# Sixteen key projections of an attention moved into the Mamba stage before it, with the first transfers reordered

## The chip, the cores and the metric

The kernel runs on one core of one Trainium2 chip, as one launch. The metric is the device time of that launch in microseconds (us), lower is better. Everything is float32 except a few bfloat16 operands named below. TensorE (PE) multiplies, ScalarE (ACT), VectorE (DVE) and GpSimd (POOL) do the elementwise work, and SyncE (SP) and ACT issue the transfers.

## The reference, cut to what matters

The network has four pairs of layers on `x` (4 batches, 256 tokens, 256 features); the change touches the first layer and the third. `ctx` is (4, 256, 128).

```python
# layer 0: Mamba on ctx; its output is gated by the normalised x
u = silu(causal_conv4(ctx @ in_proj.T) + conv_b)        # 256 channels
dt_low, Bm, Cm = split(u @ x_proj.T, [8, 16, 16])
dt = softplus(dt_low @ dt_proj.T + dt_b);  A = -exp(A_log)
for n in range(16):                                     # states
    h_t = exp(dt*A[n]) * h_{t-1} + dt*u*Bm[n]           # a scan over the 256 tokens
    y  += h * Cm[n]
x = x + tanh(g[0]) * (y + D*u) * silu(layernorm(x))
# layer 1: dense feed-forward (width 704) on layernorm(x)
# layer 2 (first attention): 16 heads of width 128
xn = layernorm(x);  q = rmsnorm(xn @ Wq) * gq;  k = rmsnorm(ctx @ Wk) * gk
v = ctx @ Wv;  x = x + tanh(g[1]) * softmax(q k^T / sqrt(128)) v @ Wo
# then: 16 experts, a second attention, 8 experts, a quantised layer, a layer on chosen tokens
```

The keys `ctx @ Wk` depend on inputs alone, not on the layers before.

## The kernel before

Tokens are worked on in two halves of 512 (two batches each), channels in two chunks of 128. One on-chip buffer, the arena, is divided by hand for each stage. Each engine runs a program in an order written out by hand: `tensor_program`, `scalar_program` and so on call the stages one after another. Semaphores named by event (`tick`, `at`) hold an engine until another has done something. Nothing is reordered by a scheduler, so an instruction that waits holds all that stand behind it on its engine.

**Mamba** (`mamba_pe`, `mamba_act`, `mamba_dve`, `mamba_pool`) has a beginning and then 32 steps: step s works on half s // 16 and state s % 16. The beginning: SP and ACT issue the input transfers; DVE multiplies the input projection by the four taps (L739); PE does the convolution of the first half with the products, 8 matmuls (L445); ACT applies silu (L561); PE projects (L456); ACT copies the 8 rows of dt (L568, `low`). From there follow the softplus and the first scan. The gates silu(layernorm(x)), one activation for each of 8 tiles (L573), need x's statistics (DVE, L222), and a power and a product on POOL; five of them stand between the two silus and two behind. POOL then builds the selecting matrices with one CAST (L405).

In step s, PE spreads the rows B and C of the next state over the partitions (L480, two bf16 matmuls into banks 0 and 1) and adds two earlier products into the sum y (L486, identity times a 128x512 tile, two of them). ACT copies C (L633, `Cs`), in odd steps B too (L629, `Bs`), and makes the decays of both chunks in PSUM (L645, `dA`). DVE multiplies the input (L765, `dBu`; in odd steps POOL makes chunk 1's, L412) and scans both chunks (L772). POOL multiplies states by C (L420, `HC`). There are two buffers for Cs and two for the states, so Cs of step s waits for HC of step s-2, the decays of step s stand behind it on ACT, and HC waits for the add two steps earlier. Between the steps stand the second half's conv, silu (step 5, with two loads of ACT's function table and one gate), projection, softplus (steps 8 to 14), and the first half's end (`gated`, `turned`, `added`, L719, L495, L729, steps 17 to 19).

**Dense** follows on PE; the first attention's first passes stand beside its second half. **Attention 1** has 32 passes N (half N // 16, head N % 16) of two units each. For a pass, three ahead, PE projects the keys (L986, q = 0: four 128x128 blocks, bank 7) and the queries (L983, q = 1: eight matmuls, bank 6); ACT squares and copies each out (L1021, L1022); DVE sums the squares, POOL takes the root, DVE normalises both in one instruction (L1056), and PE turns them (L1007). In every unit PE does scores (L1155), a transpose of the probabilities (L1166), their product with the context (L1175) and the result (L1186); in odd units of the first half also a joined weight (L996). DVE takes the maxima (L1263) and ACT the exponentials (L1229).

Of the kernel before, what the change touches and what calls it, by code (L numbers as in the profile page):

```python
# [8 lines left out]
BF16 = mybir.dt.bfloat16  # L9
# [3 lines left out]
P = 128  # L13
B, S, D = 4, 256, 256
# [17 lines left out]
FIRST, LAST = 25392, 29952  # L32

# [275 lines left out]
class Mamba:  # L309
# [5 lines left out]
    def __init__(self, k):  # L315
        NI, NBC = self.NI, self.NBC
        k.at = 0
# [3 lines left out]
        self.taps, self.Wc = k.place(self.TAPS, NI * P), k.place(self.TAPS, NI * P)  # L321
        self.cp = k.place(B, self.TAPS - 1 + S)
        self.U, self.DT, self.DU = k.place(2, NI, HALF), k.place(2, NI, HALF), k.place(2, NI, HALF)
        self.Y = k.place(2, NI, HALF)
        self.V, self.E = k.place(NI, HALF), k.place(NI, HALF)
        self.A = k.place(NI, self.NSTATE)
        self.low = k.place(HALF)
        self.bc3 = k.place(2, HALF, dt=BF16)
        self.part = k.place(HALF, dt=BF16)
        self.bcf = k.place(HALF)  # L330
        self.sel = k.place(NBC, P, dt=BF16)
        self.row = k.place(NBC)
        self.skip = k.place(NI, P)
        self.gate = k.place(NT, S)
        self.dBu = k.place(3, HALF)
        self.Bs = k.place(HALF)
        self.Hs, self.HC = k.place(4, HALF), k.place(4, HALF)
        self.Cs = k.place(2, HALF)

# [15 lines left out]

def mamba_sp(k, m):
# [5 lines left out]
    nc.sync.dma_start(m.taps.rearrange("p w n -> p (w n)"),  # L362
                      k.io["conv_taps"].partition_broadcast(P)).then_inc(*landed("taps_in"))
# [4 lines left out]

def constants_act(k, m):
    nc, landed = k.nc, k.s.landed  # L370
    nc.scalar.dma_start(k.cols[:, :], k.io["cols"]).then_inc(*landed("cols_in"))
    nc.scalar.dma_start(m.Wx, k.io["x_proj"]).then_inc(*landed("Wx_in"))
    nc.scalar.dma_start(m.Wdt[96:96 + m.RANK], k.io["dt_proj"]).then_inc(*landed("Wdt_in"))
    nc.scalar.dma_start(k.ident[:, :], k.io["ident"]).then_inc(*landed("ident_in"))
    nc.scalar.dma_start(k.rows[:, :], k.io["rows"].partition_broadcast(P)).then_inc(*landed("rows_in"))
    nc.scalar.dma_start(m.cp[:, 2:4, m.TAPS - 1:],
                        k.io["cT"][:, HALF:T].rearrange("p (b t) -> p b t", b=2)).then_inc(*landed("cp_in1"))

# [10 lines left out]
def mamba_pool(k, m):  # L389
# [10 lines left out]
    pool.wait_ge(*at("var", "m"))  # L400
    nc.gpsimd.tensor_tensor(k.rstd[:, :], k.rstd[:, :], k.mhalf[:, 0:NT], ALU.pow).then_inc(*tick("rstd", "m"))
    pool.wait_ge(*at("rstd", "m"))
# [35 lines left out]
def mamba_pe(k, m):  # L438
# [3449 lines left out]
```

## Time and profile before

| | us |
|---|---|
| three runs | 1082.51, 1083.87, 1084.74 |
| median | 1083.87 |
| the profiled execution | 1088.27 |
| its span, first to last instruction | 1086.9 |
| PE busy | 949.8 (87%) |
| DVE, ACT, POOL busy | 723.5, 519.2, 302.4 |
| mean granted TensorE clock | 0.948 |

The profile is one execution. A PE that is "busy" includes matmuls at the lower of its two clock levels, 1.2 GHz; the granted clock says how much of full speed (2.4 GHz) it had. A float32 matmul appears as two records. The waits of an engine count only where the work behind them sets the end. By the timeline, Mamba takes the span's first 173 us, the dense layer and the first passes of attention 1 the next 79, and attention 1's last result row starts at 575.2.

### The profile page before, as it was taken

Reading aid. Unit: us, or ns where it says so; the run is one execution under the profiler, and the core shown is the slowest. Engines: PE = TensorE matmul, PEld = TensorE weight load, DVE = VectorE, ACT = ScalarE, POOL = GpSimd, SP = SyncE. Lnnn points to the kernel's source line nnn. Section 1 sums busy time; section 2 is a strip of 40 time slices with the busy share of each in tenths; the row PEclk is TensorE's granted clock in tenths of the full one; section 3 lists DMA queues with packets and bytes.
Section 4 is the critical chain, followed back from the end, with each engine's and each line's share of the span. In section 5 each row is a group of like instructions: output and inputs, shape, how many; then the busy total and the mean of one; then the engine's idle time right before and its main releaser. Section 6 shows DMA issues by size and latency. Waiting matters only on the chain.

```text
span 1086.9 us, 15034 instructions
## 1 busy us (share of the span) xinstructions
PE 949.8 (87%) x4888; PEld 682.4 (63%) x4888; DVE 723.5 (67%) x1859; ACT 519.2 (48%) x1344; POOL 302.4 (28%) x282
## 2 busy tenths in 40 slices
PE   5876769999999999999999989878589898979587
PEld 2322224567899898888986777655355556545375
DVE  3899995235666766778676544567988955567753
ACT  3673562135666666565663344355356642132331
POOL 3566783112111112136210433325231100010110
PEclk9888899999999999999999999999699999989689
DMA  8500001010111128112201535412100003211100
GB/s 294 243 1 0 0 1 48 1 30 30 46 40 34 44 56 312 41 44 99 69 2 59 175 129 182 155 50 73 49 1 1 1 1 140 79 38 40 75 20 20
DMA packets 28356, 73.96 MB, mean 68 GB/s; under 512 B 4076, under 2 KB 5366, under 8 KB 27640
## 3 DMA queue, kind: packets, MB, share of 16 engines
q1 hardware_dynamic: 24344, 63.28, 17.1%
q0 software_dynamic: 3072, 8.39, 2.4%
q10 hardware_dynamic: 864, 1.34, 0.3%
q8 instruction: 40, 0.66, 0.3%
q14 instruction: 36, 0.29, 0.1%
HBM read 50.98 MB, written 22.02 MB: 67 GB/s over the span
## 4 chain that ended last, share of the span: by engine, by line
PE 62%; DVE 15%; issue 3%; ACT 2%; SPq 1%; DMA 1%; POOL 1%; another core or an unknown queue 0%; DVEq 0%; ACTq 0%
PE psum L2093 5%; PE psum L983 5%; PE psum L1694 5%; PE psum L1175 4%; PE psum L1186 4%; PE psum L844 4%; PE psum L1155 4%; PE psum L986 3%; PE psum L1166 2%; PE psum L855 2%; PE psum L1708 2%; PE psum L1007 2%; PE psum L2112 2%; PE psum L2356 2%; PE psum L2714 2%
## 5 line engine op out<-in xcount | busy, mean ns | idle before, releaser
L1065 POOL TENSOR_TENSOR arena<-arena,mhalf 128x8 f32<-128x8 f32 x32 | 54.0, 1687 | 247.6 <-DVE arena L1050 247.6
L1287 DVE SCALAR_TENSOR_TENSOR X<-psum,arena,X 128x256 f32<-128x256 f32 x128 | 55.9, 478 | 66.0 <-PE psum L1186 63.8
L420 POOL TENSOR_TENSOR arena<-arena 128x512 f32<-128x512 f32 x64 | 82.6, 1315 | 7.3 <-DVE arena L772 6.6
L772 DVE TENSOR_TENSOR_SCAN arena<-psum,arena 128x512 f32<-128x512 f32 x64 | 74.7, 1209 | 9.6 <-ACT psum L645 8.4
L1229 ACT ACTIVATE arena<-psum,arena 128x256 f32<-128x256 f32 x128 | 60.0, 477 | 34.7 <-DVE arena L1266 32.4
L1694 PE MATMUL psum<-arena 128*128 x248 | 66.5, 391 | 10.8 <-DVE arena L1789 8.9
L2375 ACT ACTIVATE arena<-psum,arena 128x240 f32<-128x240 f32 x128 | 57.3, 463 | 33.9 <-DVE arena L2389 17.0
L486 PE MATMUL psum<-arena,ident 128*128 128x512 f32 x128 | 71.5, 681 | 1.0 <-POOL arena L420 0.7
L1186 PE MATMUL psum<-arena 128*128 128x256 f32 x256 | 66.0, 380 | 1.2 <-DVE X L1287 1.1
L1175 PE MATMUL psum<-arena 128*128 128x256 f32 x256 | 65.8, 380 | 0.0
L1155 PE MATMUL psum<-arena 128*128 128x256 f32 x256 | 65.8, 380 | 0.0
L2093 PE MATMUL psum<-xT,arena 128*128 128x512 f32 x128 | 62.2, 627 | 1.3 <-ACT arena L3158 1.2
L983 PEld LDWEIGHTS psum<-arena,xT 128*128 128x128 f32 x512 | 61.9, 192 | 1.4
L1800 DVE COPY arena<-psum 128x256 f32<-128x256 f32 x62 | 26.2, 422 | 54.7 <-PE psum L1708 42.0
L983 PE MATMUL psum<-arena,xT 128*128 128x128 f32 x512 | 62.3, 275 | 0.0
L239 POOL TENSOR_TENSOR rstd<-rstd,mhalf 128x4 f32<-128x4 f32 x14 | 14.7, 1053 | 161.5 <-DVE rstd L232 161.5
L480 PE MATMUL psum<-arena 96*128 96x512 bf16 x64 | 22.5, 434 | 38.2 <-DVE arena L765 35.7
L1021 ACT ACTIVATE arena<-psum 128x512 f32<-128x512 f32 x64 | 38.3, 598 | 35.0 <-PE psum L983 18.0
L1694 PEld LDWEIGHTS psum<-arena 128*128 128x128 f32 x248 | 42.7, 192 | 18.1 <-issue 14.7
L1241 ACT COPY arena<-psum 128x512 f32<-128x512 f32 x64 | 37.6, 588 | 33.6 <-PE psum L1166 32.4
L1155 PEld LDWEIGHTS psum<-arena 128*128 128x128 f32 x256 | 48.2, 190 | 6.6 <-issue 0.3
L2714 PE MATMUL psum<-ident,arena 128*128 128x128 f32 x256 | 38.7, 293 | 15.6 <-DVE arena L2863 6.1
(359 smaller groups left out, 2296.0 us busy)
## 6 DMA issues: line engine op xcount, KB each, us to landing
arena<-in_w SPq DMA_DIRECT2D x32, 384.0 KB, 3.1
tokens<-arena SPq DMA_DIRECT2D x2, 4096.0 KB, 23.6
arena<-tokens SPq DMA_DIRECT2D x32, 256.0 KB
results<-arena SPq DMA_DIRECT2D x32, 256.0 KB
arena<-in_moe SPq DMA_DIRECT2D x17, 384.0 KB, 3.1
arena<-in_moe SPq DMA_DIRECT2D x4, 1536.0 KB, 13.6
arena<-in_w SPq DMA_DIRECT2D x2, 1024.0 KB, 6.0
arena<-in_gu SPq DMA_DIRECT2D x1, 1280.0 KB, 6.7
```

The source lines that it names most:

```text
L420: nc.gpsimd.tensor_tensor(m.HC[:, v, :], m.Hs[:, v, :], m.Cs[:, s % 2, :], ALU.mult).then_inc(*tick("HC", s, c))
L486: nc.tensor.matmul(bank[m.bank_Y[h][c]], k.ident[:, :], m.HC[:, 2 * (s % 2) + c, :], start=False, stop=n == NSTATE - 1).then_inc(*tick("y_ ...
L772: nc.vector.tensor_tensor_scan(m.Hs[:, 2 * (s % 2) + c, :], bank[m.bank_dA[c]], input_of(m, s, c), 0.0, ALU.mult, ALU.add).then_inc(*tick( ...
L983: mm = nc.tensor.matmul(bank[b][:, j * P:(j + 1) * P], k.xT[:, c, t * P:(t + 1) * P], m.W[:, p, c * P:(c + 1) * P], start=c == 0, stop=c = ...
L1155: mm = nc.tensor.matmul(bank[w][:, j * S:(j + 1) * S], m.Q[:, N % 2, i * S + j * P:i * S + (j + 1) * P], m.K[:, N % 2, i * S:(i + 1) * S], ...
L1175: mm = nc.tensor.matmul(bank[4][:, 0:S], m.ctok[:, 2 * m.batch(u) + c, :], m.PT[:, u % 2, c, :], start=c == 0, stop=c == 1)
L1186: mm = nc.tensor.matmul(bank[5][:, j * D:(j + 1) * D], m.Z[:, u % 2, j * P:(j + 1) * P], m.M[:, h, :], start=True, stop=True)
L1229: e = nc.scalar.activation(m.Pr[:, w, j, :], bank[w][:, j * S:(j + 1) * S], ACT.Exp, bias=m.nb[:, w, j:j + 1], scale=m.SCALE, accum_out=m. ...
L1694: mm = nc.tensor.matmul(bank[b][:, 0:D], m.xgT[:, n % 2, c, :], m.W[:, bass.ds(place + c * D, D)], start=c == 0, stop=c == DC - 1)
L2093: mm = nc.tensor.matmul(bank[b], m.W[:, slot, which, c * P:(c + 1) * P], k.xT[:, c, cols], start=c == 0, stop=c == DC - 1)
L2375: nc.scalar.activation(pr[:, a, 0:KM], v[:, a, 0:KM], ACT.Exp, bias=m.nb[:, u, a:a + 1], scale=m.SCALE, accum_out=m.sums[:, a % 2, places[ ...
L2714: mm = nc.tensor.transpose(bank[4 + w][:, c * S + j * P:c * S + (j + 1) * P], m.Pr[:, u, 2 * w + j, c * P:(c + 1) * P], k.ident[:, :])
```

## The change

1. The 1 MB matrix `Wk` is loaded to the chip (`key_weights_sp`, an additional input) behind the zeroing of the token buffers, into `m.Wk`.
2. The keys of the first half, 4 token tiles by 4 groups of 4 heads, are projected by 16 matmuls of 128x512 in Mamba's steps 11 to 14, 20 to 23 and 26 to 31 (two in 26 and in 29), and each is copied by ACT one step later into `Kr`, which stays on chip. The banks are those of y: the second half's y (banks 6, 7) is started in step 16 instead of 12, and the first half's (4, 5) are free from step 20.
3. In attention 1, passes 0 to 15 have no key projection and no copy of keys; ACT squares from `Kr`, and DVE normalises keys and queries in two instructions.
4. The taps are the first transfer of ACT's queue instead of the third of SP's; `ident` goes ahead of `x_proj`, and the second half of `cT` ahead of `rows`.
5. PE does 11 matmuls of 128x128 on constants before it waits for the first input (`awake`).
6. x's statistics in Mamba are finished in two halves. Two gates stand between the first silus and one behind; two stand in step 5 and three in step 17, the latter with two table loads of its own. In steps 5 and 17 all of this stands behind the decays of the step instead of ahead of them, and Cs of the next step stands behind that step's decays.
7. Buffers of U, DT, DU and Y are one for each half, so that `Kr` can lie over those of the first half; `zeros` moves.

```diff
+        self.keys = {11: [(3, 0)], 12: [(3, 1)], 13: [(3, 2)], 14: [(3, 3)], 20: [(0, 0)], 21: [(0, 1)], 22: [(0, 2)],
+                     23: [(0, 3)], 26: [(1, 0), (1, 1)], 27: [(1, 2)], 28: [(1, 3)], 29: [(2, 0), (2, 1)],
+                     30: [(2, 2)], 31: [(2, 3)]}
@@ mamba_sp
-    nc.sync.dma_start(m.taps.rearrange("p w n -> p (w n)"),
-                      k.io["conv_taps"].partition_broadcast(P)).then_inc(*landed("taps_in"))
+def key_weights_sp(k, m):
+    for h in range(2):
+        k.sp.wait_ge(*k.s.at("e_zeroed", "m1", h))
+    k.nc.sync.dma_start(m.Wk, k.io["wk1"]).then_inc(*k.s.landed("wk_in"))
@@ mamba_pool
-    pool.wait_ge(*at("var", "m"))
-    nc.gpsimd.tensor_tensor(k.rstd[:, :], k.rstd[:, :], k.mhalf[:, 0:NT], ALU.pow).then_inc(*tick("rstd", "m"))
+    for h in range(2):
+        half = slice(HT * h, HT * h + HT)
+        pool.wait_ge(*at("var", "m", h))
+        nc.gpsimd.tensor_tensor(k.rstd[:, half], k.rstd[:, half], k.mhalf[:, 0:HT], ALU.pow).then_inc(
+            *tick("rstd", "m", h))
...
@@ mamba_pe
+    def awake(b, n):
+        for _ in range(n):
+            nc.tensor.matmul(bank[b][:, 0:P], k.phalf[:, :], k.phalf[:, :], start=True, stop=True)
+    def keys(s):
+        for t, g in m.keys.get(s, ()):
+            p = 4 * t + g
+            b = m.bank_Y[s < 16][p % 2]
+            pe.wait_ge(*at("wk_in"))
+            pe.wait_ge(*at("cT_in"))
+            before = key_before(m, p)
+            if before is not None:
+                pe.wait_ge(*at("a1_K", before))
+            elif s < 16:
+                pe.wait_ge(*at("rectified", 1, 1 - p % 2))
+            else:
+                pe.wait_ge(*at("x_m", p % 2))
...
+            nc.tensor.matmul(bank[b], k.cT[:, t * P:(t + 1) * P], m.Wk[:, g * 512:(g + 1) * 512], start=True,
+                             stop=True).then_inc(*tick("a1_Kps", p))
+    pe.wait_ge(*at("halves"))
+    awake(7, 11)
     pe.wait_ge(*at("cp_in0"))
...
             rows_of(s + 1)
+        keys(s)
@@ mamba_act
+    def keys(s):
+        for t, g in m.keys.get(s, ()):
+            p = 4 * t + g
+            act.wait_ge(*at("a1_Kps", p))
+            nc.scalar.copy(m.Kr[:, t, 4 * g:4 * g + 4, :], bank[m.bank_Y[s < 16][p % 2]].rearrange(
+                "p (h d) -> p h d", h=4)).then_inc(*tick("a1_K", p))
...
-        if s == 5:
-            for c in range(NI):
-                silu(1, c)
-            gate(range(7, NT))
...
         for c in range(NI):
             act.wait_ge(*at("DT", h, c))
...
+        if s == 5:
+            for c in range(NI):
+                silu(1, c)
+            gate(range(3, 5))
+            act.wait_ge(*at("rows_in"))
+            nc.scalar.activation(k.tg[:, :], k.row("g"), ACT.Tanh).then_inc(*tick("tg"))
+        elif s == 17:
+            gate(range(5, NT))
+        if s in (5, 17):
+            nc.scalar.preload_act_table_set("natural_log_exp_and_others")
+        if s in (6, 18):
+            spread_c(s)
+        keys(s - 1)
@@ a1_project_pe
+    if N < m.NH and not q:
+        return
@@ a1_projected_act
+    if N < m.NH and not q:
+        act.wait_ge(*at("a1_K", 11))
...
+        nc.scalar.activation(m.sq[:, q, :, :], m.Kr[:, :, N, :], ACT.Square).then_inc(*k.s.tick("a1_R", N, q))
+        return
```

The programs' rows follow; each is one instruction or several alike, and the line numbers are those of the file they are from. First TensorE in attention 1, one pass of the first half before: L1155 scores, L1007 the turning of keys and queries, L1166 the transpose, L986 the keys' projection, L1175 the product with the context, L983 the queries' projection, L1186 the result.

```order
L1155 MATMUL psum<-arena 128x256 x2
L1007 MATMUL psum<-ident,arena 128x128 x8
L1166 MATMUL psum<-ident,arena 128x128 x4
L986 MATMUL psum<-arena,cT 128x128 x4
L1175 MATMUL psum<-arena 128x256 x2
L983 MATMUL psum<-arena,xT 128x128 x8
L1186 MATMUL psum<-arena 128x256 x2
```

The same stretch of TensorE in the changed kernel (L1257, L1095, L1268, L1277, L1071, L1288 are the same lines there):

```order
L1257 MATMUL psum<-arena 128x256 x2
L1095 MATMUL psum<-ident,arena 128x128 x8
L1268 MATMUL psum<-ident,arena 128x128 x4
L1277 MATMUL psum<-arena 128x256 x2
L1071 MATMUL psum<-arena,xT 128x128 x8
L1288 MATMUL psum<-arena 128x256 x2
```

The keys' projection is gone from between the transpose and the product. Next TensorE in Mamba's steps 20 to 22 before: L480 spreads the rows of B and C, L486 adds into y.

```order
L480 MATMUL psum<-arena 128x512 x2
L486 MATMUL psum<-arena,ident 128x512 x2
L480 MATMUL psum<-arena 128x512 x2
L486 MATMUL psum<-arena,ident 128x512 x2
L480 MATMUL psum<-arena 128x512 x2
L486 MATMUL psum<-arena,ident 128x512 x2
```

And in the changed kernel (L539 spreads, L498 projects keys, L545 adds):

```order
L539 MATMUL psum<-arena 128x512 x2
L498 MATMUL psum<-arena,cT 128x512
L545 MATMUL psum<-arena,ident 128x512 x2
L539 MATMUL psum<-arena 128x512 x2
L498 MATMUL psum<-arena,cT 128x512
L545 MATMUL psum<-arena,ident 128x512 x2
L539 MATMUL psum<-arena 128x512 x2
L498 MATMUL psum<-arena,cT 128x512
L545 MATMUL psum<-arena,ident 128x512 x2
```

A key projection now stands ahead of the two adds of its step. Last ScalarE around step 5 before: L629 and L633 copy B and C, L561 the silus, L573 the gate, L639 the tanh, L645 the decays.

```order
L629 COPY arena<-psum 128x512
L633 COPY arena<-psum 128x512
L561 ACT_TABLE_LOAD
L561 ACTIVATE arena<-psum,cols 128x512 x2
L573 ACTIVATE arena<-X,shift,rstd 128x256
L639 ACTIVATE tg<-rows 128x8
L640 ACT_TABLE_LOAD
L645 ACTIVATE psum<-arena 128x2x255 x2
L633 COPY arena<-psum 128x512
L645 ACTIVATE psum<-arena 128x2x255 x2
```

And in the changed kernel (L704, L675 the copies, L711 the decays, L623, L635, L720 silu, gate and tanh):

```order
L704 COPY arena<-psum 128x512
L675 COPY arena<-psum 128x512
L711 ACTIVATE psum<-arena 128x2x255 x2
L623 ACT_TABLE_LOAD
L623 ACTIVATE arena<-psum,cols 128x512 x2
L635 ACTIVATE arena<-X,shift,rstd 128x256 x2
L720 ACTIVATE tg<-rows 128x8
L724 ACT_TABLE_LOAD
L711 ACTIVATE psum<-arena 128x2x255 x2
L675 COPY arena<-psum 128x512
```

Step 5's decays stand ahead of the tables now, and step 6's follow them directly, with the copy of C behind.

## Rows read from the trace of the kernel before

**Rows 1.** Windows: length, busy of PE, PEld, DVE, ACT, POOL; PEclk, DMA share, GB/s.
```profile
73.00:93.00 20.00, 14.98 (x28) 5.76 (x27) 19.58 (x21) 12.53 (x22) 14.80 (x12) 0.76 0.00 0
...
133.00:153.00 20.00, 13.67 (x41) 5.44 (x41) 17.19 (x20) 14.70 (x26) 17.08 (x15) 1.00 0.00 1
...
293.00:313.00 20.00, 20.00 (x131) 18.11 (x130) 12.66 (x31) 13.31 (x34) 3.27 (x2) 1.00 0.14 41
```
**Rows 2.** Timeline, TensorE in attention 1: start, us, instructions, [idle before].
```profile
301.49 1.03 PE L1155 MATMUL psum<-arena 128*128 128x256 f32 x4
...
306.69 0.60 PE L1166 MATMUL psum<-ident,arena 128*128 128x128 f32 x4
307.29 1.13 PE L986 MATMUL psum<-arena,cT 128*128 128x128 f32 x8
308.25 1.03 PE L1175 MATMUL psum<-arena 128*128 128x256 f32 x4
...
311.77 1.03 PE L1155 MATMUL psum<-arena 128*128 128x256 f32 x4
```
**Rows 3.** Timeline, TensorE beside the dense layer.
```profile
222.67 1.05 PE L986 MATMUL psum<-arena,cT 128*128 128x128 f32 x8
223.56 1.95 PE L983 MATMUL psum<-arena,xT 128*128 128x128 f32 x16
```
**Rows 4.** Timeline, Mamba's beginning.
```profile
9.20 1.54 DVE L739 TENSOR_TENSOR arena<-arena 128x256 f32<-128x256 f32 x4 [8.33 <-DMA arena<-in_conv_taps]
...
9.77 9.76 PE L445 MATMUL psum<-arena 128*128 128x512 f32 x16 [9.77 <-DVE arena L739]
...
18.35 3.60 POOL L405 CAST arena<-arena 128x4096 bf16<-128x4096 f32 x1
18.44 2.57 ACT L573 ACTIVATE arena<-X,shift,rstd 128x256 f32<-128x256 f32 x5 [1.55 <-POOL shift L403]
...
20.91 0.67 ACT L561 ACTIVATE arena<-psum,cols 128x512 f32<-128x512 f32 x1
...
22.77 0.58 ACT L568 COPY arena<-psum 8x512 f32<-8x512 f32 x1 [0.21 <-PE psum L456]
```
**Rows 5.** Transfers: issue, count, KB, us from issue to landing.
```profile
arena<-in_conv_taps SPq DMA_DIRECT2D x1, 512.0 KB, 7.3
...
arena<-in_in_proj SPq DMA_DIRECT2D x1, 128.0 KB, 3.2
```
**Rows 6.** Timeline, steps 5 and 6.
```profile
51.23 1.28 ACT L561 ACT_TABLE_LOAD   x1
...
52.52 1.27 ACT L561 ACTIVATE arena<-psum,cols 128x512 f32<-128x512 f32 x2
...
56.41 2.34 DVE L772 TENSOR_TENSOR_SCAN arena<-psum,arena 128x512 f32<-128x512 f32 x2 [4.96 <-ACT psum L645]
...
59.84 2.33 DVE L772 TENSOR_TENSOR_SCAN arena<-psum,arena 128x512 f32<-128x512 f32 x2
```
**Rows 7.** Timeline, decays of step 17, scans of step 18.
```profile
111.11 1.53 ACT L645 ACTIVATE psum<-arena 128x510 f32<-128x510 f32 x2
...
117.22 2.33 DVE L772 TENSOR_TENSOR_SCAN arena<-psum,arena 128x512 f32<-128x512 f32 x2
```
**Rows 8.** Timeline, two pairs of adds in Mamba, and DVE beside POOL.
```profile
71.78 3.62 PE L486 MATMUL psum<-arena,ident 128*128 128x512 f32 x4
...
97.79 1.63 DVE L714 TENSOR_TENSOR arena<-arena 128x512 f32<-128x512 f32 x1
...
150.28 1.88 PE L486 MATMUL psum<-arena,ident 128*128 128x512 f32 x4
```
**Rows 9.** Timeline, the end of Mamba.
```profile
163.12 0.59 ACT L629 COPY arena<-psum 128x512 f32<-128x512 f32 x1 [0.17 <-PE psum L480]
...
165.02 4.95 POOL L420 TENSOR_TENSOR arena<-arena 128x512 f32<-128x512 f32 x4
...
172.02 1.06 PE L495 MATMUL psum<-ident,arena 128*128 128x128 f32 x8 [0.88 <-DVE arena L719]
```

More of the change, by code:

```diff
@@ L316, in __init__ @@
         NI, NBC = self.NI, self.NBC
-        k.at = 0
+        k.at = KEYS1
+        self.U, self.DT, self.DU = ([k.place(NI, HALF)] for _ in range(3))
+        self.V, self.E = k.place(NI, HALF), k.place(NI, HALF)
+        self.Y = [k.place(NI, HALF)]
+        assert k.at == KEYS1 + 3 * 2048
+        self.cp = k.place(B, self.TAPS - 1 + S)
+        self.Wc = k.place(self.TAPS, NI * P)
         self.Win = k.place(NI * P)
@@ L353, in input_of, with key_before @@
     return m.dBu[:, c + c * (s % 2), :]
+def key_before(m, p):
+    order = [4 * t + g for s in sorted(m.keys) if (s < 16) == (p >= 12) for t, g in m.keys[s]]
+    same = [q for q in order[:order.index(p)] if q % 2 == p % 2]
+    return same[-1] if same else None
 def mamba_sp(k, m):
@@ L604, in mamba_act @@
     silu(0, 0)
-    gate(range(0, 5))
+    gate(range(0, 2))
     silu(0, 1)
-    gate(range(5, 7))
+    gate(range(2, 3))
     low(0)
@@ L629, in mamba_act @@
             nc.scalar.copy(m.Bs, bank[m.bank_B]).then_inc(*tick("Bs", s))
-        act.wait_ge(*at("C_ps", s))
-        if s >= 2:
-            act.wait_ge(*at("HC", s - 2, 1))
-        nc.scalar.copy(m.Cs[:, s % 2, :], bank[m.bank_C]).then_inc(*tick("Cs", s))
-        if s == 5:
-            for c in range(NI):
-                silu(1, c)
-            gate(range(7, NT))
-            act.wait_ge(*at("rows_in"))
-            nc.scalar.activation(k.tg[:, :], k.row("g"), ACT.Tanh).then_inc(*tick("tg"))
-            nc.scalar.preload_act_table_set("natural_log_exp_and_others")
+        if s not in (6, 18):
+            spread_c(s)
         for c in range(NI):
@@ L666, in mamba_act @@
             turned_act(k, "d", 0, (4, 5))
+    keys(m.UNITS - 1)
 def mamba_dve(k, m):
@@ L1055, in a1_normalise_dve @@
     v = m.R[:, N % 3]
+    if N < m.NH:
+        if N >= 3:
+            k.dve.wait_ge(*k.s.at("a1_turn", N - 3, 0))
+        for q in range(2):
+            r = m.rr[:, N % 3, q].unsqueeze(2).broadcast_to([P, HT, m.HD])
+            a = k.nc.vector.tensor_tensor(v[:, q], v[:, q] if q else m.Kr[:, :, N, :], r, ALU.mult)
+        a.then_inc(*k.s.tick("a1_N", N))
+        return
     k.nc.vector.tensor_tensor(v, v, m.rr[:, N % 3].unsqueeze(3).broadcast_to([P, 2, HT, m.HD]),
```

115 lines of the change are left out of this document (70 added, 45 removed).

## The prediction

> **What bounds the kernel now.** I read the windows first, then the timeline inside them. In a window of attention 1, PE is busy 20.00 of 20 us at clock 1.00, DVE 12.66 and ACT 13.31 [rows 1]: PE sets that stage, and work taken from PE there shortens it. In Mamba it is otherwise. In 73:93 DVE is busy 19.58 of 20 us; in 133:153 DVE and POOL have 17.19 and 17.08, PE 13.67 [rows 1]. There DVE's scans set the pace, POOL runs close behind, and PE has room. So the change takes work from where PE is full and puts it where PE is not. The timeline then prices the pieces: one pass of attention 1 [rows 2], the beginning [rows 4, 5], the tables [rows 6, 7] and the end of Mamba [rows 9].
>
> **Keys out of attention 1.** A pass lasts 10.28 us (301.49 to 311.77) [rows 2]. Ahead of the key projection stand four transpose records, from 306.69. Back-to-back records of that size start 0.11 apart: the projection's own eight would take 0.87. So the transposes are through at 306.69 + 0.43 = 307.12, the projection starts at 307.29 and the next product at 308.25: 1.13 us in all, 0.87 of work and 0.26 of gaps before and behind it. Beside the dense layer it is 223.56 - 222.67 = 0.89 [rows 3]. The change removes 16: 3 beside the dense layer, 13 in attention 1. 3 x 0.89 + 13 x 1.13 = 17.4 if the gaps go too, 16 x 0.87 = 13.9 if they move to the next instruction. I take 17.0, since the other joints in this stretch show no gap.
>
> Is PE still the bound then? The pass would be 9.15 us. DVE has 12.66 / 20 x 10.28 = 6.5 of it, and some 0.15 more, as the normalisation becomes two instructions; ACT has 6.8, and one copy of about 0.6 less. Both leave 2.5 us. In the short, odd unit nothing changes: there the key projection never stood. In the long, even unit the transpose of the next unit comes about 1.1 us earlier, but ACT also has its exponentials 0.6 earlier (the copy is gone). The queue gap that remains is larger than what moved, so I count no new wait.
>
> **The beginning.** The path is taps landed, DVE's products, 16 conv records, silu, projection, `low` at 22.77 [rows 4].
> - Taps: third in SP's queue, they were issued at 1.9 and landed 7.3 later [rows 5], just ahead of DVE's 9.20 [rows 4]. They now go first in ACT's queue, at about 0.73, the time at which that queue's first transfer went out. Their flight is between 3.2 (the 128 KB beside them) and 7.3 [rows 5]. Half way, 5.3 (an estimate), gives 6.1 instead of 9.20: 3.1 us, between 1.2 and the 4.6 at which in_proj, which DVE also needs, lands (1.38 + 3.2).
> - Conv: 16 records took 9.76 [rows 4], the first six 0.86 apart at the lower level, the rest 0.43. At full clock all would take 6.9: 2.8 less. So full speed came some 5.2 us (6 x 0.86) after PE's first record. `awake` starts at about 1.2 and, at 22 records of 0.21 (a quarter of 0.86, an estimate), runs to 5.9, so the conv at 6.4 could well be at full speed. I take 2.4, bounds 0 and 2.8.
> - Gates: before, five gates held the second silu until 20.91, though the conv was through at 19.5; from there `low` followed 1.86 later. Now two gates stand there. They need x's first half, its statistics and a power on POOL, by my count at about 12.3, and end at 13.3, just as the conv ends. The 1.4 us go, between 0 (x late) and 1.4.
> - Against it: POOL's CAST of 3.6 us [rows 4] came before DVE's work behind `low`, and would now stand beside it. The trace has DVE instructions with two inputs on chip at 1.63 beside POOL [rows 8], though the same instruction takes 0.69 alone. I charge 0.5.
> The sum is 3.1 + 2.4 + 1.4 - 0.5 = 6.4 us earlier; bounds 2.5 and 8. From `low` to the first scan nothing else changes.
>
> The Trainium skill (SBUF — State Buffer, the rule on the shared port pair) says that a DVE instruction with two SBUF inputs and a GpSimd one lock each other out for the whole instruction. By that rule the CAST could hold DVE for up to its full 3.6 us, and the beginning would give 3.1 less than I say; the 1.63 above fits the rule, but the instructions that would meet the CAST come before a PE wait and have slack.
>
> **Step 5.** Before, table, silus, gate, tanh and table stood ahead of the decays: DVE's scan waited 4.96 until 56.41, and step 6's began at 59.84 [rows 6]. Now the decays of step 5 begin at 51.2 (where the table began) and end at 52.5. Then 1.28 + 1.27 + 2 x 0.53 + 0.2 + 1.28 = 5.1 gives 57.6, and step 6's decay 0.69 more: its scan starts at 58.3. So the wait does not go, it moves one step: 59.84 - 58.3 = 1.5 gained, bounds 0 and 3. Copy and `low` of step 6 come later on ACT, but they are due only after that scan.
>
> **Step 17.** Added: two tables and three gates, 2.56 + 1.5 = 4.1, behind decays that end at 112.64. 116.75 plus a decay of 0.69 is 117.45; step 18's scan started at 117.22 [rows 7]. I charge 0.3, bounds 0 and 1.5. What hides the 4.1 is DVE's own work in that step. The later copies on ACT delay POOL's next by 0.8, and two steps further DVE's work on x gives POOL time again.
> The Trainium skill (ScalarE: Activation LUTs, What ACT_TABLE_LOAD costs) adds a drain of some 1.38 us to each load of 1.28. The trace disagrees: the silu starts at 52.52, right behind the load of 51.23 + 1.28 [rows 6]. With the drain, step 17 would cost 2.8 more.
>
> **Keys in Mamba.** 16 matmuls of 0.87 at full clock (two records of 0.43, as the adds [rows 8]) and 1.7 at the lower level, and 16 ACT copies of 0.59 [rows 9].
> - PE: a step has rows 0.6 and two adds 1.73, so 2.3; with a key 3.2, with two 4.1. A pair of steps on DVE takes two times two scans in 2.34 [rows 6] and three products of 0.65, 6.6, so 3.3 each. PE just fits, and one step with two keys is made good in the next. Steps 11 to 14 last 5 to 6 us each, because DVE has softplus there: those four cost nothing.
> - What stands behind a key on PE is the two adds, which POOL's product two steps on waits for; behind a key copy on ACT stands Bs of the next step, and POOL is nearly full: five instructions, 6.2 of each 6.6. In steps 22 to 25 Cs already waits for POOL and the scan for ACT, so 0.6 of delay per copy shows, about 1.0 in all. At the end, step 30's two copies put Bs (163.12) off by 1.0, POOL's last four (165.02, 4.95) follow, and after them the turn at 172.02 [rows 9]: 1.0. For steps 20 and 26 to 29 I add 0.5.
> I take 2.5; bounds 0 (all hidden, no gain is possible) and 7 (0.6 for each of the 12 late copies).
> `Wk` is due in step 11, at some 76 us; its load waits for the zeroing, whose transfers end before 50. In SP's queue only the first attention's weights stand behind it, and those wait for Mamba's end anyway.
>
> **The sum.** -17.0 - 6.4 - 1.5 + 0.3 + 2.5 = -22.1 us. Against the profiled execution's own 1088.27 (span 1086.9, 1.4 around it) that is 1066.2. The three timed runs have a median 4.4 lower, 1083.87, and the stages named have no part that differs between executions as far as I can see, so the forecast is 1083.87 - 22.1 = 1061.8.
>
> **The rivals.**
> 1. Attention 1 is held by the loop scores, maxima, exponentials, transpose, and not by PE's work. For it: ACT waits 0.6 for DVE there now and then, DVE's odd unit has 3.8 us of work to PE's 3.5. Against: PE shows no idle time. Then the 13 passes give 0.3 each instead of 1.13, 11 us less gain: 1073. Chance 0.07.
> 2. Mamba's last twelve steps lose more than I charge, as POOL is nearly full and every copy delays it: 7 to 10 instead of 2.5, 1066 to 1069. Chance 0.14.
> 3. The beginning gives little: the taps land late as ACT's and SP's queues share the same engines, and PE's clock has fallen again by the time they do. 6.4 becomes 2: 1066. Chance 0.09.
> 4. The other side: in steps 20 to 31 PE is granted the lower level. Then a step is 1.0 + 1.7 + 3.4 = 6.1 on PE (four add records in 3.62, against 1.88 [rows 8]), 2.8 above DVE's 3.3, and twelve steps lose 34 us less my 2.5: 1093. Before, steps 9 to 14 ran at clock 0.76, but 133:153 at 1.00 [rows 1], and more work on PE speaks for the upper level. It decides from 2.1 us per step. Chance 0.03.
> The forecast's case keeps 0.67.
>
> **Range.** The forecast's own case is 1058 to 1065 (13.9 against 17.4 for the keys, 4 to 8 for the beginning). Rivals 2 and 3 reach to 1069. I give 1057 to 1068; above it lie rival 1, rival 4 and the tail of 2. Faster by over 0.2% (2.2 us, what a measurement here can tell from no change) 0.95, the same 0.02, slower 0.03: only rival 4, or several losses at once, undo 22 us.
>
> **What would show it.** In the profile after: conv records 0.43 apart from the first, and `low` near 16.4; the scan of step 6 waiting about 2.9 for ACT, step 5's hardly; step 18's scan waiting 0.3; PE's clock 1.00 in steps 21 to 31, and PE's turn of the last y about 5.2 us earlier (172.02 to about 166.9); the pass of attention 1 at 9.15 with PE 20 of 20. If PE shows waits for ACT in the even units, the keys' term is wrong; if DVE waits for ACT or PE in steps 20 to 31 more than 3 us over before, the Mamba term is.

## The result, and the profile after

| | before | after |
|---|---|---|
| median of 4 runs on one chip, us | 1083.19 | 1065.13 |
| their spread | 1081.37 to 1084.74 | 1060.83 to 1066.05 |
| ratio, 95% interval | | 0.9829, 0.9805 to 0.9853 |
| span of the profiled execution | 1086.9 | 1063.9 |

The kernel became faster by 18.1 us by the medians and by 23.0 between the two profiled executions (22.1 forecast). Before's profiled execution, 1088.27, was slower than each of its four timed runs, so the 23.0 flatters the change. The forecast of the median was 1061.8, 3.3 below what was measured. How much earlier each landmark comes than before, by the timelines of the two kernels:

| landmark | before | after | earlier by | forecast |
|---|---|---|---|---|
| first scan | 34.55 | 28.23 | 6.32 | 6.4 |
| scan of step 4 | 48.09 | 41.99 | 6.10 | |
| scan of step 6 | 59.84 | 51.99 | 7.85 | 7.9 |
| scan of step 7 | 64.74 | 57.83 | 6.91 | 7.9 |
| scan of step 16 | 109.59 | 100.36 | 9.23 | 7.9 |
| scan of step 18 | 117.22 | 108.36 | 8.86 | 7.6 |
| PE's turn of the last y | 172.02 | 165.44 | 6.58 | 5.1 |
| attention 1, last result begins | 575.2 | 554.5 | 20.7 | 22.1 |
| end of span | 1086.9 | 1063.9 | 23.0 | 22.1 |

The windows of after (columns as in [rows 1], the same three stretches) show PE still full in attention 1, and busier at clock 1.00 late in Mamba: 17.25 us instead of 13.67.

```profile
73.00:93.00 20.00, 14.28 (x29) 5.31 (x30) 19.72 (x22) 11.16 (x19) 14.27 (x11) 0.83 0.00 0
133.00:153.00 20.00, 17.25 (x52) 7.62 (x51) 19.25 (x23) 15.21 (x27) 18.43 (x16) 1.00 0.00 0
293.00:313.00 20.00, 20.00 (x131) 18.30 (x130) 14.97 (x35) 13.37 (x36) 3.27 (x2) 1.00 0.15 50
```

**The beginning**, against [rows 4]. Timeline of after: start, us, instruction, [idle before].

```profile
1.20 4.91 PE L480 MATMUL psum<-phalf 128*128 128x128 f32 x22 [1.20 <-POOL phalf L416]
...
6.86 1.55 DVE L820 TENSOR_TENSOR arena<-arena 128x256 f32<-128x256 f32 x4 [5.99 <-DMA arena<-in_in_proj]
...
7.43 7.11 PE L504 MATMUL psum<-arena 128*128 128x512 f32 x16 [1.32 <-DVE arena L820]
...
13.54 3.60 POOL L440 CAST arena<-arena 128x4096 bf16<-128x4096 f32 x1
...
16.45 0.58 ACT L630 COPY arena<-psum 8x512 f32<-8x512 f32 x1 [0.71 <-PE psum L515]
```

The products begin 2.34 us earlier and now wait for `in_proj`, not for the taps. The convolution takes 7.11 instead of 9.76, with the 22 matmuls of `awake` (11 of float32, two records each) ending 1.32 before it. POOL's CAST is over before DVE's next instruction, at 17.14: it collides with nothing there.

**Step 6 and step 7.** DVE in after: the wait of 4.96 [rows 6] is now 2.75, one step later, and in step 7 a cast that took 0.55 in before takes 1.48: POOL's products (55.60, 2.67 for both) begin 0.06 ahead of it.

```profile
51.99 2.34 DVE L855 TENSOR_TENSOR_SCAN arena<-psum,arena 128x512 f32<-128x512 f32 x2 [2.75 <-ACT psum L711]
...
55.66 1.48 DVE L767 CAST arena<-arena 96x512 bf16<-96x512 f32 x1
...
57.83 2.34 DVE L855 TENSOR_TENSOR_SCAN arena<-psum,arena 128x512 f32<-128x512 f32 x2
```

**Step 11**, where I had counted nothing. First before, then after. In before DVE's product of two arrays on chip (L706) takes 1.64, while POOL's second product is at work.

```profile
84.10 3.22 PE L486 MATMUL psum<-arena,ident 128*128 128x512 f32 x4
...
86.16 1.42 POOL L420 TENSOR_TENSOR arena<-arena 128x512 f32<-128x512 f32 x1 [0.25 <-PE psum L486]
...
86.49 1.64 DVE L706 TENSOR_TENSOR arena<-arena 128x512 f32<-128x512 f32 x1
```
```profile
76.62 1.04 PE L498 MATMUL psum<-arena,cT 128*128 128x512 f32 x2
77.48 3.57 PE L545 MATMUL psum<-arena,ident 128*128 128x512 f32 x4
...
79.36 0.69 DVE L787 TENSOR_TENSOR arena<-arena 128x512 f32<-128x512 f32 x1
...
79.51 1.67 POOL L455 TENSOR_TENSOR arena<-arena 128x512 f32<-128x512 f32 x1 [0.73 <-PE psum L545]
```

The key projection (L498) stands ahead of the adds on PE, and POOL's second product waits for an add. So it comes 0.15 behind DVE's product instead of 0.33 ahead of it, and now DVE has 0.69 and POOL the 1.67. Step 13 shows the same: 0.95 us each. Not every trace has this gain; the run with the keys behind the adds, below, says which.

**Steps 18 and 22, and Mamba's end**, against [rows 7, 9].

```profile
108.36 2.34 DVE L855 TENSOR_TENSOR_SCAN arena<-psum,arena 128x512 f32<-128x512 f32 x2 [0.18 <-ACT psum L711]
...
127.26 2.34 DVE L855 TENSOR_TENSOR_SCAN arena<-psum,arena 128x512 f32<-128x512 f32 x2 [2.48 <-ACT psum L711]
...
165.44 1.06 PE L554 MATMUL psum<-ident,arena 128*128 128x128 f32 x8 [0.87 <-DVE arena L800]
```

**Attention 1**, against [rows 2]: its first unit, one pass from score to score, and the first pass of the second half.

```profile
248.14 3.65 PE L1071 MATMUL psum<-arena,xT 128*128 128x128 f32 x16 [0.59 <-ACT arena L1131]
...
283.41 1.03 PE L1257 MATMUL psum<-arena 128*128 128x256 f32 x4
...
292.56 0.81 PE L1257 MATMUL psum<-arena 128*128 128x256 f32 x3
...
408.62 1.16 PE L1074 MATMUL psum<-arena,cT 128*128 128x128 f32 x8 [0.96 <-DMA arena<-in_w]
```

(The view ends at 293, so the row of 292.56 counts three of its four records.) A pass takes 292.56 - 283.41 = 9.15, and 12 of them give 1.12 or 1.13 each. Two joints are new: in the first unit the queries wait 0.59 for ACT and run at the lower level for most of it (3.65 instead of 1.95), and at the second half PE waits 0.96 for a weight (0.25 before).

### The profile page after: what moved, and what is told of

The parts are those of the page before. It is cut to its first block, busy times and chain, and to the rows that moved or that the text cites. A ratio compares the mean times of both kernels' runs of the same rounds, so it can differ in the third digit from the quotient of the medians.

```text
span 1063.9 us, 14909 instructions
## 1 busy us (share of the span) xinstructions
PE 947.4 (89%) x4814; PEld 678.0 (64%) x4814; DVE 724.5 (68%) x1877; ACT 521.4 (49%) x1346; POOL 303.0 (28%) x284
## 4 chain that ended last, share of the span: by engine, by line
PE 63%; DVE 15%; issue 3%; ACT 2%; DMA 1%; SPq 1%; POOL 1%; DVEq 0%; POOLq 0%; ACTq 0%
PE psum L2195 5%; PE psum L1071 5%; PE psum L1796 5%; PE psum L1277 4%; PE psum L1288 4%; PE psum L927 4%; PE psum L1257 4%; PE psum L1268 2%; PE psum L938 2%; PE psum L2458 2%; PE psum L2816 2%; PE psum L1810 2%; PE psum L1095 2%; PE psum L2214 2%; PE psum L2834 2%
## 5 line engine op out<-in xcount | busy, mean ns | idle before, releaser
L545 PE MATMUL psum<-arena,ident 128*128 128x512 f32 x128 | 68.2, 658 | 0.1
L1288 PE MATMUL psum<-arena 128*128 128x256 f32 x256 | 65.9, 380 | 1.2 <-DVE X L1389 1.1
L1277 PE MATMUL psum<-arena 128*128 128x256 f32 x256 | 65.8, 380 | 0.0
L1257 PE MATMUL psum<-arena 128*128 128x256 f32 x256 | 65.8, 380 | 0.0
L1071 PEld LDWEIGHTS psum<-arena,xT 128*128 128x128 f32 x512 | 63.3, 196 | 3.9 <-issue 2.1
L1071 PE MATMUL psum<-arena,xT 128*128 128x128 f32 x512 | 64.1, 280 | 0.6 <-ACT arena L1131 0.6
L1796 PEld LDWEIGHTS psum<-arena 128*128 128x128 f32 x248 | 42.7, 192 | 18.0 <-issue 14.4
L1257 PEld LDWEIGHTS psum<-arena 128*128 128x128 f32 x256 | 48.2, 190 | 6.6 <-issue 0.3
L1288 PEld LDWEIGHTS psum<-arena 128*128 128x128 f32 x256 | 46.3, 190 | 7.0 <-issue 1.4
L1131 ACT ACTIVATE arena<-psum,cols 128x512 f32<-128x512 f32 x64 | 40.5, 685 | 19.6 <-PE psum L1095 19.5
```

What stands on the lines that cost most here:

```text
L545: nc.tensor.matmul(bank[m.bank_Y[h][c]], k.ident[:, :], m.HC[:, 2 * (s % 2) + c, :], start=False, stop=n == NSTATE - 1).then_inc(*tick("y_ ...
L1071: mm = nc.tensor.matmul(bank[b][:, j * P:(j + 1) * P], k.xT[:, c, t * P:(t + 1) * P], m.W[:, p, c * P:(c + 1) * P], start=c == 0, stop=c = ...
L1257: mm = nc.tensor.matmul(bank[w][:, j * S:(j + 1) * S], m.Q[:, N % 2, i * S + j * P:i * S + (j + 1) * P], m.K[:, N % 2, i * S:(i + 1) * S], ...
L1277: mm = nc.tensor.matmul(bank[4][:, 0:S], m.ctok[:, 2 * m.batch(u) + c, :], m.PT[:, u % 2, c, :], start=c == 0, stop=c == 1)
L1288: mm = nc.tensor.matmul(bank[5][:, j * D:(j + 1) * D], m.Z[:, u % 2, j * P:(j + 1) * P], m.M[:, h, :], start=True, stop=True)
L1796: mm = nc.tensor.matmul(bank[b][:, 0:D], m.xgT[:, n % 2, c, :], m.W[:, bass.ds(place + c * D, D)], start=c == 0, stop=c == DC - 1)
```

## The experiments

Landmarks are given, as above, by how much earlier they are than in before's trace. A single time says little, since executions of one kernel differ by several us (after's four by 5.2); the traces are what tells the theories apart.

### Keys back in attention, the rest of the change kept (3 rounds)

```diff
-        self.keys = {11: ... 31: [(2, 3)]}
+        self.keys = {}
-    key_weights_sp(k, st.mamba)
```
Attention 1 projects, copies and normalises as before.

> The changed kernel with the keys of the first half projected in attention 1 again (none in Mamba, no load of Wk, y of the second half begun in step 12 as before); start, tables and gates stay changed. Theory: of the 23.1 us between the two profiled spans the keys account for 14: 3 x 0.9 beside the dense layer and 12 x 1.13 in attention 1, less 1.3 lost at its first unit and 0.7 at a wait for weights, less 0.4 in Mamba (2.3 lost late, 1.9 gained in steps 11 to 14). Span about 1063.9 + 14 = 1078, ratio to the kernel before about 0.992. The first scan stays at 28.2, the scans of step 20 begin at about 120.1 instead of 118.2. Rival (the keys gave the 17 less 2.5 that was forecast, and the 1.9 in steps 11 to 14 has another cause): the scans of step 20 stay at 118.2.

Measured: 1079.79 against 1083.29, ratio 0.9966 (0.9952 to 0.998); profiled span 1077.6. The span is what was expected (1078), the ratio is nearer to 1 than the 0.992 expected. Its scans stand within 0.02 us of after's from the first to step 11. From there it lacks the gain: the scan of step 16 is 7.15 earlier (after 9.23). Up to the last turn it loses little: 6.6 earlier (after 6.58). At the end of attention 1 it is 6.9 earlier, after 20.7. So the keys give 13.8 us, all of it beyond Mamba: in Mamba they gain 2.1 in steps 11 to 16 and lose as much in the late ones. By the medians the other parts of the change give 3.5 us where the trace has 6.9, so the medians fall short of the traces without the keys, too.

### No `awake` in the beginning

```diff
-    pe.wait_ge(*at("halves"))
-    awake(7, 11)
```

> The changed kernel without the 11 small matmuls at the start. Theory: the first conv's 16 records run at the lower level for their first 5.2 us, end 2.6 later, and the first scan begins at 30.5 to 30.8 instead of 28.2; all behind follows by as much. Rival (the conv is at full speed anyway, or the silus wait for the gates instead): first scan within 0.5 of 28.2.

Measured: 1068.38. The first scan comes at 30.59 instead of 28.23, as expected.

```profile
7.24 9.65 PE L504 MATMUL psum<-arena 128*128 128x512 f32 x16 [7.24 <-DVE arena L818]
```

PE had done nothing before it, and 16 records took 9.65 instead of 7.11. The term exists: 2.4 us. But two other kernels with the same beginning as after's show it only in part: in the one with a filled first unit and the copy-free one (both runs of it, below) the convolution took 8.80, 8.78 and 8.59, though `awake` ended 1.92, 1.03 and 1.25 ahead of it. In seven executions of six kernels it took 7.11. So the 22 matmuls do not buy full clock in every kernel.

### Taps in SP's queue, behind `in_proj`

```diff
-    nc.scalar.dma_start(m.taps..., k.io["conv_taps"]...)      # first in ACT's queue
     nc.sync.dma_start(m.Win, k.io["in_proj"])
+    nc.sync.dma_start(m.taps..., k.io["conv_taps"]...)
```

> The changed kernel with the taps third in SP's queue as before (the rest of the order of transfers stays). Theory: they land near 9, DVE's products begin some 2.3 later than 6.86, and TensorE, idle from 6.1 on, has fallen to the lower level by then, so the conv takes up to 2.8 more: first scan at 31 to 33 instead of 28.2. Rival (the landing hangs on what the two queues carry together, not on the place): products still begin within 0.5 of 6.9.

Measured: 1070.18. Timeline of its first 20 us:

```profile
8.47 1.43 DVE L820 TENSOR_TENSOR arena<-arena 128x256 f32<-128x256 f32 x4 [7.60 <-DMA arena<-in_conv_taps]
...
9.04 9.66 PE L504 MATMUL psum<-arena 128*128 128x512 f32 x16 [2.77 <-DVE arena L820]
```

The products come 1.6 later (2.3 expected), the first scan 4.2 (32.39, within what was expected): the rest is the clock, which was down after a gap of 2.77. So 1.6 of transfer order carries 2.5 of clock with it.

### Step 5's tables ahead of the decays again

```diff
+        if s == 5:
+            silus, gate, tanh, table      # ahead of the decays, as before
```

> The changed kernel with the tables, silus, gates and tanh of step 5 ahead of its decays again, as before the change, with its two gates. Theory: the scan of step 5 waits some 5.5 and that of step 6 follows without a wait, so it begins 1.5 + 0.5 (the second gate) = 2.0 later than with the change, at about 54.0 where all else agrees; of it 0.9 is gone by step 7, since ACT's dt copy and POOL are late in the changed kernel and not here. Rival (the wait has only moved, nothing gained): within 0.5 of 52.0.

Measured: 1067.03. DVE's scans of steps 5 to 7:

```profile
49.87 2.34 DVE L855 TENSOR_TENSOR_SCAN arena<-psum,arena 128x512 f32<-128x512 f32 x2 [5.46 <-ACT psum L718]
...
53.29 2.33 DVE L855 TENSOR_TENSOR_SCAN arena<-psum,arena 128x512 f32<-128x512 f32 x2
...
58.20 2.34 DVE L855 TENSOR_TENSOR_SCAN arena<-psum,arena 128x512 f32<-128x512 f32 x2
```

Step 4 began 0.94 ahead of after's in this execution, step 6 1.30 behind it, step 7 0.37 behind. So the new order is worth 2.24 at step 6, and 1.31 once step 7 has given back 0.93 (2.0 and 0.9 expected). L767 takes 0.56 here at 56.96, ahead of the same scan: the cast of 1.48 comes with the new order.

### Keys behind the adds in steps 11 to 14

```diff
-        keys(s)                  # ahead of the adds, in all steps
+        if s >= 16: keys(s)
...
         add(s - 1, 0)
+        if s < 16: keys(s)
```

> The changed kernel, the four key projections of steps 11 to 14 behind the two adds of their step on TensorE instead of ahead of them. Theory (the key holds up the add, the add holds up POOL's product, and DVE's instruction with two inputs on chip starts before POOL's and takes 0.69 instead of 1.64): steps 11 and 13 lose 0.95 each, and the scans of step 16 begin at 102.3 instead of 100.4. Rival (TensorE works more and has the higher clock, so rows come sooner): as much work stands in each step, the scans of step 16 stay within 0.3 of 100.4.

Measured: 1065.15. In step 11 POOL's two products run on (77.34, 2.94 for both), DVE's has 1.64 (79.19), and the scan of step 16 begins at 102.06, 7.5 earlier than before where after has 9.23. So the order on PE is needed: the adds ran at the lower level here too (2.67, and 3.48 in step 13), and without a key ahead of them nothing was gained.

It is not enough. Ten profiled executions have a key ahead of the adds. Of their 20 steps 11 and 13, 12 gained the 0.95, and in each of these the key or the adds ran at least in part at the lower level, as in after's step 11. In the other eight the key took 1.02 and the adds 1.88, and nothing was gained: in both steps of the kernels without `awake`, with the taps in SP's queue and with the norms later (below), and in one step each of the filled kernel and the one with the tables ahead. Step 11 with the norms later, on PE, POOL and DVE:

```profile
76.80 1.02 PE L498 MATMUL psum<-arena,cT 128*128 128x512 f32 x2
77.66 1.88 PE L545 MATMUL psum<-arena,ident 128*128 128x512 f32 x4
...
77.69 2.93 POOL L455 TENSOR_TENSOR arena<-arena 128x512 f32<-128x512 f32 x2 [0.86 <-DVE arena L855]
...
79.53 1.64 DVE L787 TENSOR_TENSOR arena<-arena 128x512 f32<-128x512 f32 x1
```

At full clock the key puts the adds off by 0.86, POOL runs on without a wait, and DVE pays. So 1.9 us of after's gain hang on slow matmuls in these two steps.

### Before, with only a delay on PE

```diff
+        if s in (11, 12, 13, 14):      # in the kernel before, ahead of the adds
+            for _ in range(4):
+                nc.tensor.matmul(bank[7][:, 0:P], k.phalf[:, :], k.phalf[:, :], ...)
```
The second half's y starts in step 16, to leave bank 7 free.

> The kernel before, with y of the second half begun in step 16, and 4 small matmuls on constants (0.9 us at full clock, nothing reads them) ahead of the adds of steps 11 to 14: a delay, and no work of the change. Theory (the gain of 1.9 us in steps 11 to 14 comes from the delay of POOL alone): the scans of step 16 begin at 107.7 instead of 109.59. Rival (it comes from something else in the change): 109.6 or later.

Measured: 1084.98. PE, DVE and POOL in step 11:

```profile
83.58 1.87 PE L518 MATMUL psum<-phalf 128*128 128x128 f32 x8
85.25 2.77 PE L486 MATMUL psum<-arena,ident 128*128 128x512 f32 x4
...
86.33 0.69 DVE L710 TENSOR_TENSOR arena<-arena 128x512 f32<-128x512 f32 x1
...
87.30 1.27 POOL L420 TENSOR_TENSOR arena<-arena 128x512 f32<-128x512 f32 x1 [1.56 <-PE psum L486]
```

The four matmuls, planned as 0.9, ran at the lower level and put the adds off by 1.67. Matmuls whose result nobody reads make Mamba shorter: step 16's scan is at 107.32 against 109.59, with 0.2 of this there by step 11. 1.9 us come from steps 11 and 13 (0.69 at 96.68 too), as in after. This shows the cause: which of DVE and POOL comes first. The whole kernel took 1084.98 and before 1081.10, one run each, so a gain of the whole is not shown.

### The first unit of attention filled (3 rounds)

```diff
+        if u == 0: filled(6)       # 128x128 matmuls into bank 4
         transposed(u)
+        if u == 0: filled(3)
```

> The changed kernel with 6 and 3 small matmuls on constants (bank 4, nothing reads them) ahead of and behind the first transpose in attention 1, where TensorE waits 1.32 and 0.59 us. Theory (the idle time let the clock fall to the lower level, so that the 16 records of the next projection took 3.65 instead of 1.95): they take 1.95, and the rest of the kernel comes 1.7 earlier, span about 1062.2. Rival (the projection is slow for another reason, such as waiting for operands): no change, 1063.9.

Measured: 1066.25, ratio 0.9835 (0.981 to 0.986), no better than after. The queries took 2.02 instead of 3.65, but so they did in seven other executions of kernels without the filling (2.02 each). 3.65 stood in after and 3.62 in its repeat, 2.88 with the tables ahead. So this run doesn't show that the filling does anything.

### Norms of x one step later

```diff
-        elif s in (21, 22):        # ACT's layernorm of x for the dense layer
+        elif s in (22, 23):
```

> The changed kernel with the four normalising activations of ACT in steps 22 and 23 instead of 21 and 22. In step 21 ACT waits 3.28 for POOL's shift with the decays of step 22 behind it, and that scan waits 2.48. Theory: the wait on ACT goes, and the scan of step 22 begins 1.5 to 2.5 earlier than 127.26; of it 1 to 2 remain at the end of Mamba (TensorE's turn of y at 165.44 before). Rival (POOL is the bound in these steps and Cs waits for it anyway): under 0.5 remains at the end.

Measured: 1059.31, span 1058.0. DVE's scans of steps 20 to 22, and PE's turn:

```profile
120.49 2.33 DVE L855 TENSOR_TENSOR_SCAN arena<-psum,arena 128x512 f32<-128x512 f32 x2
...
123.49 2.34 DVE L855 TENSOR_TENSOR_SCAN arena<-psum,arena 128x512 f32<-128x512 f32 x2
...
126.92 2.33 DVE L855 TENSOR_TENSOR_SCAN arena<-psum,arena 128x512 f32<-128x512 f32 x2
```

The wait of 2.48 at step 22 is gone. In after ACT's norm stands ahead of Cs and the decays and waits 3.28 for POOL's statistics; here they are ready. From the scan of step 20 to the turn it is 44.41 us (after 47.22), 2.8 less. Before had a wait of 1.90 there already, so most of this cost is older than the change. The 0.6 more that after has is not the key's copy. From the scan of step 20 to that of step 22 it is 8.42 in before and 9.04 in after, 9.08 and 9.04 in the kernel without the copies, but 8.41 to 8.42 in three kernels that have them (no `awake`, taps in SP's queue, keys behind). What goes with it is TensorE's level in step 20: after 3.73 of idle PE the key there took 1.91 in after and without the copies, after 2.22 it took 1.02 in the three others, and here 1.02 too. Against those three (46.60 from the scan of step 20 to the turn) the edit gives 2.2 of the 2.8. Of the 5.9 us by which this run beats after's profiled one, only 2.6 stand at the end of attention 1; the rest came in the experts. In 700:860 this execution had a granted clock of 0.96 (after 0.90), but the repeat of after below had 0.93 there and still ended later than after, so the clock isn't shown to be the reason.

### Late key copies left out (twice)

```diff
             act.wait_ge(*at("a1_Kps", p))
+            if s >= 16: continue           # no copy of 12 of the 16 keys
             nc.scalar.copy(...)
```
The heads of these 12 keys read what lay there; what waited for a copy waits for the projection.

> The changed kernel without ACT's copies of the 12 late keys (heads then read what lay there before; TensorE projects them all the same). Theory (of the 2.3 us that Mamba's steps 20 to 31 lose, the copies on ACT are the cause: they stand ahead of the copy of B and of the decays): 1.8 to 2.3 come back by TensorE's turn of the last y, 165.44 to about 163.4. Rival (TensorE is the cause: the keys hold up the adds): under 0.7 comes back.

> The same kernel as e8 (the 12 late copies of keys left out, so heads read what lay there), since in e8 TensorE had the lower level in step 26. Theory: with full clock from step 21 on, the scans of step 31 begin 1.0 to 1.5 earlier against those of step 20 than in the changed kernel (40.0 between them there), and the last turn 1.8 earlier. Rival (the adds held up by the keys on TensorE are the cause): under 0.5.

Measured: 1066.71 and 1063.19. Neither gives back what was expected. In the second, with its first scan 1.58 behind after's, the scan of step 23 follows that of step 22 by 3.17 instead of 3.65, as in before (3.16), and steps 23 to 27 take as long as after's: 0.5 is what copies cost there. Then step 28 loses 1.33, and the turn comes 2.5 behind after's. Step 26 on PE and DVE:

```profile
143.53 3.51 PE L498 MATMUL psum<-arena,cT 128*128 128x512 f32 x4
146.83 1.99 PE L545 MATMUL psum<-arena,ident 128*128 128x512 f32 x4
...
149.08 1.28 DVE L850 TENSOR_TENSOR arena<-arena,psum 128x512 f32<-128x512 f32 x2 [0.80 <-PE psum L539]
```

Its two keys took 3.51 instead of 1.88, after 1.88 of idle PE, and DVE waited for PE. The first run has 3.38 in the same place. This is my rival 4 in one step, where POOL and ACT had less to do. So the runs put the copies' cost in steps 22 to 27 at 0.5. Behind the last scan they cost next to nothing: from the scan of step 31 to the turn it is 7.14 and 7.13 here, 7.20 in after and 6.47 in before.

### After again, and after with two edits (5 rounds, same chip)

The repeat is the changed kernel, unaltered. The other has the norms one step later and 28 `awake` matmuls instead of 22:

```diff
-        elif s in (21, 22):
+        elif s in (22, 23):
-    awake(7, 11)
+    awake(7, 14)
```

> The changed kernel once more, word for word. Theory (what TensorE's clock is granted in Mamba differs between executions, and terms of the change hang on it): the conv's 16 records take either 7.1 or some 8.8, and the adds of step 11 take 3.6 with the second input instruction of DVE at 0.69, or 1.9 with it at 1.64; the runs spread over some 5 us around 1065. Rival (the differences between the traces come from the edits of the experiments): this trace agrees with the first within 0.3 us at every mark, 7.11, 3.57 and 0.69.

> The changed kernel with the normalising activations one step later (as in e7) and 14 small matmuls at the start instead of 11, so that they end at 7.2 at the latest, just before the conv, and leave no idle time. Theory: the conv always takes 7.1 (0 to 1.7 gained, by the execution) and the scan of step 22 loses no 2.5 (2.0 gained, of which 0.5 to 2.0 stay at Mamba's end): 1 to 3 us below the changed kernel in the median, 1062 to 1064. Rival (later stages' clocks cover it): within 1 us of it.

| 6 runs each | median | lowest, highest | ratio to before (median 1085.37) |
|---|---|---|---|
| after again | 1068.72 | 1063.58, 1071.14 | 0.9828 (0.979 to 0.9867) |
| two edits | 1064.29 | 1061.12, 1068.94 | 0.9800 (0.9762 to 0.9839) |

The repeat's profiled execution stands within 0.15 us of after's from the first scan to the last result of attention 1, and ends 3.4 later: all that differs between the two came behind 559. The theory was that terms of the change differ between executions, the rival that the differences between the traces go with the edits. The rival's marks came: 7.11, 3.52 for the adds, 0.69. The copy-free kernel, the only other one profiled twice, says the same. Its two executions agree within 0.07 at every scan and within 0.4 at the end of attention 1, with the long convolution and the slow keys of step 26 in both, and behind attention 1 they differ by 3.9. So a level was never seen to change between two executions of one kernel in the stages touched. Why kernels whose programs are equal up to a stage ran it at different levels isn't shown.

The version with two edits turns its last y at 162.00 (after 165.44) and ends attention 1 5.7 earlier: 2.6 from the wait at step 22, 1.6 from queries at full level in the first unit (2.02), 0.7 from steps 3 and 4, where the granted clock was higher (0.89 in 20:50, after 0.84), 0.7 from a wait for the second half's weight of 0.28 instead of 0.96. Only the first is what an edit was meant to do, and of it 0.6 is the level in step 20, where the key took 1.02 as with the norms later. Its convolution took 7.11, as with 22 matmuls, so the second edit shows nothing. The median is 4.4 below that of the repeat, but the two intervals overlap: faster by the trace up to attention's end, not proved over the whole kernel.

## Why the prediction was right, and where it was not

- **Size and sum.** -22.1 was forecast; the profiled spans say -23.0, the landmark behind attention 1 -20.7. The medians say -18.1, and -16.6 in the later runs. Part of the nearness is luck: attention 1 gave 2.9 less than forecast, and all ahead of it 1.5 more (6.58 against 5.1), mostly by steps 11 and 13, where I had counted nothing. I took 22.1 off the lower median and wrote that the stages named "have no part that differs between executions". The two kernels profiled twice bear that out up to the end of attention 1. What differs lies behind it: there, where the change does nothing, the fourteen profiled executions took 505.9 to 513.2, and the same kernel differed by 3.4 and 3.9. What makes the medians' gain 2 to 4 less than the 20.7 isn't settled: before was profiled once only.
- **Beginning, 6.4: measured 6.32**, from other pieces. The taps term was 3.1, got 2.34, since `in_proj` lands behind them. The conv term of 2.4 got 2.65. The gates gave what was left (1.3), and the 0.5 charged for CAST beside DVE did not arise: it ended at 17.14 as DVE began. The Trainium skill's rule (SBUF — State Buffer, on the shared port pair) was weighed at the wrong place: the trace agrees with it in steps 11 and 13 (0.69 and 1.67 where DVE began first, 1.64 where POOL did).
- **Step 5, 1.5: measured 1.75 at step 6**, of which 0.94 went back at step 7: its cast fell just behind POOL's product and took 1.48. The wait of 2.75 was forecast as 2.9. I had ended the account at step 6's scan; it should have run until the engines stood in their old order again.
- **Step 17, 0.3: measured 0.37**, the wait 0.18. In step 5 too the decays start at 51.27, right behind a load of 1.28 at 49.97. The drain that the Trainium skill adds to each load (ScalarE: Activation LUTs, What ACT_TABLE_LOAD costs) shows in neither.
- **Keys in Mamba, 2.5: measured 2.28 late**, but 1.9 gained in steps 11 and 13, a gain for which my bounds "0 (all hidden, no gain is possible)" left no room. That reason was false: work added ahead of the adds changed who comes first, and the run with a bare delay shows it. It took the lower level, too: where TensorE ran these steps at full clock the gain is missing. Of the late loss 0.6 goes with the lower level in step 20, 0.5 is copies, in step 23, where I had about 1.0 for the copies. 1.2 comes from step 30 on (1.0 forecast), 0.7 of it behind the last scan, and there it is not the copies, as the kernel without them shows; what it is stays open. Rival 2 (7 to 10) did not come. Rival 4 came in single steps: step 20 of after, step 26 where copies were left out.
- **Keys out of attention, 17.0: measured 14.1** at its end, 13.8 against the version with keys put back. The unit price was right: 0.89 to 0.99 beside the dense layer, 1.12 to 1.13 in 12 passes, 16.2 in all. The sixteenth key, that of attention 1's first unit, brought a loss of 1.3 there instead of a gain, and the second half's first weight cost 0.7. My "I count no new wait" held for the steady passes and failed at the two joints. In the first unit 1.6 is the lower level: eight executions had the queries at 2.02 there, and from the last turn to the end of attention 1 they took 386.7 to 387.4, that is 16.0 to 16.7 less than before's 403.4 (after 14.1). PE remained the bound, so rival 1 falls.

## What to carry to other kernels

Price a moved piece per instruction, as was done here, but look separately at the joints of the stage it leaves: the first unit and the next weight lost 2 us in after that 12 steady passes did not show. Where two engines meet in time, ask which comes first with and without the change, since an order can flip at 0.3 us of shift (DVE paid when POOL began 0.15 ahead, and not when it began 0.15 behind) and a forecast of "hidden, so nothing" has no bound on either side. Check a forecast at landmarks of the stages touched: the end of a span had 3.4 and 3.9 us in it between two executions of one kernel. And before a difference between two traces is called chance or is put down to an edit, profile one kernel twice and look for the same mark in all other traces: the 0.6 at step 22 looked like a copy's cost until the kernels without copies showed it as well.

## What the runs showed of the hardware

- DVE's product of two 128x512 arrays on chip took 0.69 or 1.64, POOL's 1.27 or 1.67, by which began first (POOL 0.33 ahead in before, 0.15 behind in after). Useless matmuls that delay POOL gained 1.9 us. The rule of the Trainium skill named above fits these rows.
- So slower matmuls made Mamba shorter: with the key and the adds of steps 11 and 13 at full clock (1.02 and 1.88) none of eight steps gained the 0.95, with one of them at the lower level all of 12 did.
- The same beginning gave a convolution at full speed in seven executions (7.11) and not in three (8.59 to 8.80), with PE idle for 0.90 to 1.83 us ahead of it in the former and 1.03 to 1.92 in the latter. The gap alone doesn't tell them apart. The two kernels profiled twice had 7.11 both times, and 8.78 and 8.59. Without `awake` it took 9.65.
- In step 26 PE was idle for 1.88 us, and its two keys took 3.38 and 3.51 in the copy-free runs; in after it was idle for 1.83 there and they took 1.88.
- The second half's first weight was waited for between 0.21 and 0.96 us in ten executions with the keys moved, by no time that shows in the eleventh (the filled kernel), and 0.25 in before.
